# Two attention layers on one core: the first passes' q and k copied straight from the part tile, and TensorE's first scores ahead of the second half's k, v and sums

## The chip, the cores and the metric

The kernel runs on one core of a Trainium2 chip. The metric is the device time of one execution in microseconds. The profile is one execution taken by the hardware profiler; the times named in the text are microseconds from the start of its span.

## The reference, cut to what matters

The input x is (4, 1024, 128) in float32: batch, rows, features. Two attentions with 16 heads of 8 features follow each other, then a choice of 2 of 8 experts.

```python
def _L0_attn_ref(x, Wqkv, bqkv, Wr, br):        # first attention, on _layernorm(x)
    qkv = jnp.einsum('bhce,ef->bhcf', xh, Wqkv) + bqkv
    q, k, v = jnp.split(qkv, 3, axis=-1)
    att = jnp.einsum('bhqe,bhke->bhqk', q, k) / jnp.sqrt(jnp.float32(he))
    mask = jnp.tril(jnp.ones((c, c), dtype=att.dtype), k=-1)
    att = jax.nn.softmax(att * mask, axis=-1)   # masked scores are 0, not -inf
    out = jnp.einsum('bhqk,bhke->bhqe', att, v)
    ...
    return out @ Wr + br
...
    # second attention: rope on q and k inputs, causal softmax, out_proj, layer norm,
    # gates, top 2 of 8 experts, layer norm
x = x + _L0_attn_ref(_layernorm(x, axis=-1), ...)
x = x + _L0_ffn_ref(_layernorm(x, axis=-1), ...)
```

Since the masked scores of the first attention are 0 and not left out, every query also needs the sum of v over all later keys: that is the `suffix` job ("the sums").

## The kernel before, in words

**Slots, stretches, passes, sets, units.** An attention of one batch is a slot; `SLOTS` gives their order, the first attention of batch 0, then of batch 1, then the second attention of batch 0, and so on. A stretch is the stream of scores of one slot. It runs in passes: one half of the queries (512) by four of the 16 heads; the first four passes are those of the first query half. A pass is a row of sets, each set one or two units. A unit is a 128 x 1024 block of scores in a pair of PSUM banks; there are three pairs (`PAIRS`), so unit n uses the banks of unit n - 3. In the first query half a pass has three sets of 2, 2 and 1 units, so set 0 has units 0 and 1, set 1 has 2 and 3, set 2 has 4, set 3 begins pass 1.

**The stream.** For each set TensorE computes scores (line 1309, `heads_scores`), ScalarE takes the exponential of a unit (line 1504), GpSimd masks the blocks on the diagonal (line 1580), and three sets later (`LAG`) TensorE multiplies by v (line 1334, `value_group`). ScalarE copies a pass' result out (line 1429). q and k of a pass lie in `qs` and `ks`, three buffers each (`RING`), signalled by `qs_in`.

**Side work.** Everything else (norms, projections, the second attention's inputs, experts) is cut into turns such as `("p1", 1, "xT", 0)`: work, batch, name, half (p1: the first attention's q, k, v; p2: its output and the second's q, k, v; p3: what follows). A planner, `schedule()`, runs at build time with estimated lengths (`JOB_TIMES`, `TURN_TIMES`) and a clock for each engine, and puts each turn at a point between sets, two points in a set. Every engine carries out its turns in this order, in its own stream, and waits where data isn't there: a turn that waits on TensorE or GpSimd holds up the scores or masks behind it. PSUM results of TensorE jobs are counted by `side_done` and, once read, by `side_free`.

**The front.** What must be ready before the first scores is in a list by hand, `BEFORE_TURNS`, of batch 0: for both row halves j = 0, 1 the statistics (`stats`, `root`), normalised rows (`rows`), transpose (`xT`), `q`, `k`, the stores to DRAM (`parts_out`) and `v`; then the two `suffix` sums; between them `pairs`, `bound` and `roots` of p0, a bound on the scores that ends in a flag, which each engine but GpSimd reads before a stretch. TensorE does all its jobs of the list, then waits for `N_SCORES` reads and for pass 0's data, and begins. Each q and k is split in two float32r parts in the tile `part` (lines 1675 and 1676; for k of this list ScalarE makes the first part, line 1441, and VectorE the second). `parts_out` stores q in four DMAs and k in two; for half 0 the k stores are ScalarE's (line 919). Then SP loads passes 0 and 1 from DRAM (`load(0)`, `load(1)`; it waits until all six stores have landed), where q's parts are each stored twice, and k is read twice, because the scores are products of parts on 64 rows for each head.

**The queues of the front.** SP issues the first rows, `FIRST`, `bv` and `WEIGHTS`, then the turns. ScalarE issues the `NARROW` loads, converts them, then issues `BROADCAST` (eight vectors, then `earlier8` and `bars8`), `cos` and `sin`, and only then carries out its turns, the first of them `roots`.

## Time and profile before

| | |
|---|---|
| median of 3 runs | 789.04 us (788.24 to 795.55) |
| the profiled execution's own time | 789.42 us |
| its span | 787.6 us |
| TensorE matmul, busy | 681.1 us (86%) |
| ScalarE, busy | 648.1 us (82%) |
| VectorE, busy | 395.9 us (50%) |
| GpSimd, busy | 322.9 us (41%) |

The exponentials (128 x 1024, 576 of them, 1124 ns each) are 601.4 us of ScalarE's time; the products with v 322.2 us and the scores 185.1 us of TensorE's. The page also cuts the span into 40 slices of 19.7 us and gives each engine's busy share in tenths:

```profile
PE   4798998988899989989897989989999789999853
PEld 2333333433234333233232333233333233233422
DVE  5355344456445453556244644574345765455573
ACT  1499997999899997999698889998889798888721
POOL 3162235323633434434553245532666314424334
PEclk9589998999999997999898999999999999999976
```

ScalarE (ACT) is busy in one tenth of the first slice, four of the second, and then nine or so until the last slices. PEclk is TensorE's granted clock, in tenths of full speed. A timeline row reads: start, length, engine, line, operation, output and inputs with their shapes, number of merged instructions, and in square brackets the idle time before and what released it.

### The profile page before, as it was taken

The numbers are of one execution on the slowest core, as the hardware profiler recorded it, in microseconds if no ns is written. First come the engines' busy times: TensorE is split into PE (matmuls) and PEld (weight loads), VectorE is DVE, ScalarE is ACT, GpSimd is POOL, SyncE is SP. The second block draws the span as 40 slices with busy tenths as digits, with TensorE's granted clock in tenths as the row PEclk, the third lists the DMA queues.
The fourth block names the chain that finished last, engine by engine and source line by source line (L and its number), as shares of the span: only waits on it lengthen the run. The fifth ranks groups of instructions, "written<-read, shape, count | busy, mean of one in ns | idle before, by whom it ended". The sixth has DMA issues, their size and how long they took to land. (4 is left out here: it accounts for less than half of the span.)

```text
span 787.6 us, 15418 instructions
## 1 busy us (share of the span) xinstructions
PE 681.1 (86%) x5568; PEld 259.9 (33%) x5568; DVE 395.9 (50%) x1062; ACT 648.1 (82%) x721; POOL 322.9 (41%) x635
## 2 busy tenths in 40 slices
PE   4798998988899989989897989989999789999853
PEld 2333333433234333233232333233333233233422
DVE  5355344456445453556244644574345765455573
ACT  1499997999899997999698889998889798888721
POOL 3162235323633434434553245532666314424334
PEclk9589998999999997999898999999999999999976
DMA  6848357535567432424455244423545451230100
GB/s 162 288 136 263 101 202 239 178 127 202 181 213 243 162 110 86 148 83 135 143 163 155 104 141 130 146 83 121 190 151 179 158 162 60 70 96 1 41 13 15
DMA packets 77142, 109.86 MB, mean 139 GB/s; under 512 B 13928, under 2 KB 28400, under 8 KB 77040
## 3 DMA queue, kind: packets, MB, share of 16 engines
q1 hardware_dynamic: 72944, 107.32, 42.8%
q10 hardware_dynamic: 4096, 1.33, 0.8%
q8 instruction: 46, 0.75, 0.4%
q14 instruction: 56, 0.46, 0.2%
HBM read 60.94 MB, written 47.68 MB: 138 GB/s over the span
## 5 line engine op out<-in xcount | busy, mean ns | idle before, releaser
L1504 ACT ACTIVATE probs<-scores,shift 128x1024 f32<-128x1024 f32 x576 | 601.4, 1124 | 80.2 <-PE scores L1309 73.7
L1580 POOL TENSOR_SCALAR_AFFINE_SELECT probs<-probs 128x256 f32<-128x256 f32 (+1 forms) x448 | 197.5, 458 | 379.8 <-ACT probs L1504 379.1
L1334 PE MATMUL acc<-probs,v 128*9 128x512 f32 (+3 forms) x3072 | 322.2, 508 | 10.7 <-ACT num L1429 9.5
L1309 PE MATMUL scores<-qs,ks 32*128 32x512 f32 (+3 forms) x1536 | 185.1, 434 | 41.0 <-ACT probs L1504 37.4
L1309 PEld LDWEIGHTS scores<-qs,ks 32*128 32x128 f32 x1536 | 83.1, 189 | 259.9 <-ACT probs L1504 175.0
L1334 PEld LDWEIGHTS acc<-probs,v 128*9 128x9 f32 x3072 | 59.1, 100 | 132.2 <-issue 72.9
L1627 DVE TENSOR_TENSOR prod<-side,G 128x512 f32<-128x512 f32 x48 | 33.1, 691 | 89.3 <-PE side L1275 79.3
L1275 PE MATMUL side<-we,x1T 128*128 128x512 f32 x100 | 58.6, 669 | 0.8 <-DVE x1T L1916 0.8
L1561 POOL TENSOR_TENSOR moe<-psum 128x256 f32<-128x256 f32 x32 | 24.4, 762 | 51.3 <-DVE x1b L1627 26.6
L1429 ACT ACTIVATE num<-acc 128x512 f32<-128x512 f32 x64 | 38.2, 596 | 5.3 <-PE acc L1334 5.2
L1536 POOL TENSOR_TENSOR rstd<-rstd,expo 128x4 f32<-128x4 f32 x32 | 33.4, 1044 | 2.7
L1660 DVE COPY xT<-side 128x512 f32<-128x512 f32 x22 | 15.2, 691 | 30.2 <-PE side L1148 30.1
L1675 DVE TENSOR_SCALAR part<-side,binqk 128x512 fp32r<-128x512 f32 x16 | 12.0, 751 | 31.4 <-PE side L1154 21.8
L1154 PE MATMUL side<-xT,win 128*128 128x512 f32 x32 | 20.1, 712 | 6.6 <-DVE part L1676 6.6
L1464 ACT ACTIVATE probs<-scores,G 128x128 f32<-128x128 f32 x40 | 11.0, 389 | 15.4 <-PE scores L1275 9.9
L1675 DVE TENSOR_SCALAR part<-side,bqk 128x512 fp32r<-128x512 f32 x12 | 9.0, 751 | 25.0 <-PE side L1154 25.0
L1635 DVE BATCH_NORM_STATS2 stats<-xrow 128x6 f32<-128x128 f32 x72 | 15.6, 279 | 11.8 <-DMA xrow<-in_x 9.5
L1275 PEld LDWEIGHTS side<-we,x1T 128*128 128x128 f32 x100 | 15.5, 195 | 16.1 <-issue 11.4
L1627 DVE TENSOR_TENSOR psum<-prod 128x512 f32<-128x512 f32 x24 | 17.7, 737 | 3.1
L1275 PE MATMUL scores<-we,x1T 128*128 128x512 f32 x28 | 17.4, 767 | 0.0
L1562 POOL TENSOR_TENSOR moe<-moe 128x128 f32<-128x128 f32 x32 | 15.8, 493 | 2.5
L1848 DVE TENSOR_SCALAR sfx<-side,sfx 128x128 f32<-128x128 f32 x28 | 9.8, 351 | 12.6 <-PE side L1235 8.4
(186 smaller groups left out, 602.4 us busy)
## 6 DMA issues: line engine op xcount, KB each, us to landing
ks<-k_dram SPq DMA_DIRECT2D x96, 256.0 KB, 4.1
q_dram<-part SPq DMA_DIRECT2D x64, 256.0 KB, 3.5
qs<-q_dram SPq DMA_DIRECT2D x64, 256.0 KB, 3.2
num_dram<-num SPq DMA_DIRECT2D x60, 256.0 KB, 3.3
k_dram<-part SPq DMA_DIRECT2D x30, 256.0 KB, 4.0
xrow<-in_x SPq DMA_DIRECT2D x16, 256.0 KB, 4.4
nat<-num_dram SPq DMA_DIRECT2D x15, 256.0 KB
rdenb<-rden_dram SPq DMA_DIRECT2D x15, 256.0 KB
```

What stands on the lines that cost most here:

```text
L1154: signal(pe.matmul(out[:, :], w[:, int(name == "k"), :], xT[a][:, a or j, :], start=True, stop=True), last)
L1275: signal(pe.matmul(out[:, :], x1T[i // TH][:, i % TH, :], we[:, first:first + HALF], start=True, stop=True), last)
L1309: ins = pe.matmul(dst, ks[u][r, kt // TH, (kt % TH) * P:(kt % TH + 1) * P], qs[u][r, q0:q0 + w], start=True, stop=not shifted)
L1334: ins = pe.matmul(acc[h * VW:h * VW + VC, q0:q0 + w], v9[V_OF[k]][:, kt, :, HG * hg + h], src, start=(s == 0), stop=last, skip_group_check ...
L1429: act.activation(num[gp % 2][:, :], acc[:, :], ACT.Copy).then_inc(acc_read, 1)
L1504: act.activation(dst, src, ACT.Exp, bias=shift[:, column(st):column(st) + 1], scale=SCALE).then_inc(probs_raw, 1)
L1536: pool.tensor_tensor(r, r, expo[:, 0:1].broadcast_to(list(r.shape)), ALU.pow).then_inc(root_ready[w], 1)
L1561: link(pool.tensor_tensor(moe[:, :, :], psum4[:, i % 2, 0:2, :], psum4[:, i % 2, 2:4, :], ALU.add))
L1562: link(pool.tensor_tensor(moe1[:, :], moe[:, 0, :], moe[:, 1, :], ALU.add))
L1580: ins = pool.affine_select(out=blocks, in_=blocks, compare_op=ALU.is_ge, fill=0.0, base=a - 1, pattern=[[0, blocks.shape[1]], [1, P]], cha ...
L1627: return dve.tensor_tensor(out, in0, in1, op)
L1675: link(dve.tensor_scalar(pt[:, c, 0, :], src, bias[:, c:c + 1], None, ALU.add))
```

## The change

- The list: `rows` of half 0 stands before `pairs`, `q` of half 0 before `roots` (on VectorE).
- `STRAIGHT = 2`: passes 0 and 1 get q and k by DMA from the tile `part` (SBUF) into `qs` and `ks` (SBUF) instead of by way of DRAM. A pass takes four copies of 128 KB: two of q (SP) and two of k (one by SP, one by ScalarE). Pass 0's q copies are issued once `q` is read, the others once `k` is. The stores to DRAM stay, behind the copies; `load(2)` follows them, in place of `load(0)` and `load(1)`.
- `BEHIND`: TensorE's `k` and `v` of half 1 follow set 0's scores, the sums sets 1 and 3. The first part of `k` of half 1 is made by VectorE, not ScalarE. `BEFORE_BANKS` names the banks of the jobs in the list, and `PAIR_FREE` replaces the wait for `N_SCORES` by one for each pair: pair 0 needs `k` of half 0 to be read, pair 2 (set 1) `k` of half 1.
- `earlier8`, `bars8`, `cos` and `sin` leave ScalarE's queue for SP's, behind the second half's `parts_out`, with a semaphore of their own, for which VectorE waits at the first `rope0` and the first `pick0`.
- The planner starts VectorE's and SP's clocks at 5.0, and places no TensorE job before set 4.

```diff
@@ -349,11 +349,16 @@
-BEFORE_TURNS = ([("p1", 0, "stats", 0), ("p1", 0, "root", 0), ("p1", 0, "stats", 1), ("p1", 0, "root", 1), ("p0", 0, "pairs", 0),
-                 ("p1", 0, "rows", 0), ("p1", 0, "xT", 0), ("p0", 0, "bound", 0), ("p1", 0, "rows", 1), ("p0", 0, "roots", 0),
-                 ("p1", 0, "q", 0), ("p1", 0, "k", 0), ("p1", 0, "parts_out", 0), ("p1", 0, "xT", 1), ("p1", 0, "v", 0),
+BEFORE_TURNS = ([("p1", 0, "stats", 0), ("p1", 0, "root", 0), ("p1", 0, "stats", 1), ("p1", 0, "root", 1),
+                 ("p1", 0, "rows", 0), ("p0", 0, "pairs", 0), ("p1", 0, "xT", 0), ("p0", 0, "bound", 0), ("p1", 0, "rows", 1),
+                 ("p1", 0, "q", 0), ("p0", 0, "roots", 0), ("p1", 0, "k", 0), ("p1", 0, "parts_out", 0), ("p1", 0, "xT", 1), ("p1", 0, "v", 0),
                  ("p1", 0, "q", 1), ("p1", 0, "k", 1), ("p1", 0, "parts_out", 1), ("p1", 0, "v", 1), ("p1", 0, "suffix", 1), ("p1", 0, "suffix", 0)])
 PIECES.update(pairs=1, bound=1)
+BEFORE_BANKS = {("p1", 0, "xT", 0): 1, ("p0", 0, "pairs", 0): 0, ("p0", 0, "bound", 0): 2, ("p1", 0, "q", 0): 3, ("p1", 0, "k", 0): 0,
+                ("p1", 0, "xT", 1): 4, ("p1", 0, "q", 1): 5, ("p1", 0, "k", 1): 4}
+BEHIND = {("p1", 0, "k", 1): 0, ("p1", 0, "v", 1): 0, ("p1", 0, "suffix", 1): 1, ("p1", 0, "suffix", 0): 3}
@@ -382,7 +387,7 @@
     pending = sorted(waits, key=late)
-    clock = {"PE": 0.0, "ACT": 0.0, "DVE": 0.0, "POOL": 0.0, "SP": 0.0}
+    clock = {"PE": 0.0, "ACT": 0.0, "DVE": 5.0, "POOL": 0.0, "SP": 5.0}
     banks, jobs, uses = [0.0], [], [x for x in BEFORE_TURNS if x[2] == "q"]
@@ -493,7 +498,7 @@
         others(t, p, False)
-        room = True
+        room = g > max(BEHIND.values())
         if room and open_job is None and banks[-1] <= t and p + 4 < NPOINT:
@@ -575,7 +580,7 @@
 BY_ACT = set(BY_ACT_ORDER)
-K_BY_ACT = [x[:4] for x in BEFORE if x[2] == "k" and x[5]]
+K_BY_ACT = [x[:4] for x in BEFORE if x[2] == "k" and x[5] and x[:4] not in BEHIND]
 TURNS = [x for x in BEFORE + sum(DURING, []) + AFTER if x[5]]
@@ -594,8 +599,7 @@
 N_AFTER = sum(x[2] in PIECES and x[5] for x in AFTER)
-JOB_BANK = [n % (SPARE + 1) if n < N_BEFORE - 2 else SPARE for n in range(N_BEFORE)] + [SPARE] * (len(JOB) - N_BEFORE - N_AFTER)
+JOB_BANK = [BEFORE_BANKS.get(x, SPARE) for x in JOBS[:N_BEFORE]] + [SPARE] * (len(JOB) - N_BEFORE - N_AFTER)
 JOB_BANK += [n % (SPARE + 1) for n in range(N_AFTER)]
@@ -621,6 +625,7 @@
 N_SCORES = max(n for n in range(N_BEFORE) if JOB_BANK[n] < SPARE) + 1
+PAIR_FREE = [max(n for n in range(N_BEFORE) if JOB_BANK[n] // 2 == i) + 1 for i in range(PAIRS)]
 FIRST_FILLS = NVB + 3
@@ -854,10 +860,10 @@
         BROADCAST = [(binv, binv_d), (br, br_d), (bo, bo_d), (bg, bg_d), (l1w, l1w_d), (l1b, l1b_d),
-                     (l2w, l2w_d), (l2b, l2b_d), (earlier8, earlier8_d), (bars8, bars8_d)]
+                     (l2w, l2w_d), (l2b, l2b_d)]
         n_first = len(FIRST)
         n_narrow = len(NARROW)
-        n_weights = len(WEIGHTS) + len(BROADCAST) + 2
+        n_weights = len(WEIGHTS) + len(BROADCAST)
         PARTS_DMAS = 6
@@ -871,9 +877,21 @@
+        STRAIGHT = 2
         def landed(gp):
-            return 16 * sum(pass_dmas(i) for i in range(gp % RING, gp + 1, RING))
+            return 16 * sum(4 if i < STRAIGHT else pass_dmas(i) for i in range(gp % RING, gp + 1, RING))
+        def q_straight(engine, gp, i):
+            src = part[0][32 * gp:32 * gp + 32, 0, i, :].bitcast(F32)
+            engine.dma_start(qs[gp][i::2, :].bitcast(F32), src.unsqueeze(1).broadcast_to([32, 2, HALF])).then_inc(qs_in[gp], 16)
+        def k_straight(engine, gp, i):
+            engine.dma_start(ks[gp][i::2, 0, :].bitcast(F32), part[0][32 * gp:32 * gp + 32, 1, :, :].bitcast(F32)).then_inc(qs_in[gp], 16)
@@ -954,7 +972,7 @@
                 _st, k, qh, hg = PASS_OF[gp]
-                if hg == 0:
+                if hg == 0 or gp == STRAIGHT:
                     wait_stored(k, qh)
@@ -1084,13 +1102,25 @@
             for x in BEFORE:
+                if x[:4] == ("p1", 0, "parts_out", 0):
+                    sp.wait_ge(side_free, done(("p1", 0, "q", 0)))
+                    for i in range(2):
+                        q_straight(sp, 0, i)
+                    sp.wait_ge(side_free, done(("p1", 0, "k", 0)))
+                    k_straight(sp, 0, 0)
+                    for i in range(2):
+                        q_straight(sp, 1, i)
+                    k_straight(sp, 1, 0)
                 if x[5]:
...
                 if x[:4] == ("p1", 0, "parts_out", 0):
-                    load(0)
-                    load(1)
+                    load(2)
+            for t, d in ((earlier8, earlier8_d), (bars8, bars8_d)):
+                sp.dma_start(t[:, :], bc(d)).then_inc(late_weights_in, 16)
+            for t, d in ((cos, cos_d), (sin, sin_d)):
+                sp.dma_start(t[:, :, :], d.rearrange("(t p) f -> p t f", p=P)).then_inc(late_weights_in, 16)
             loads = {}
-            for gp in range(2, NP):
+            for gp in range(3, NP):
                 first = max(PASS_FIRST[gp] - LEAD, PASS_FIRST[gp - RING + 1] if gp >= RING else 0)
@@ -1282,10 +1312,11 @@
                     pe.wait_ge(qs_in[u], landed(gp))
-                if g == 0:
-                    pe.wait_ge(side_free, N_SCORES)
-                elif last >= PAIRS:
+                for unit in UNITS_OF[g]:
+                    if unit < PAIRS:
+                        pe.wait_ge(side_free, PAIR_FREE[unit])
+                if last >= PAIRS:
@@ -1369,8 +1400,14 @@
             for x in BEFORE:
-                turn(*x)
+                if x[:4] not in BEHIND:
+                    turn(*x)
             pe.wait_ge(narrowed, n_narrow)
+            def behind(g):
+                for x in BEFORE:
+                    if BEHIND.get(x[:4]) == g:
+                        turn(*x)
@@ -1378,6 +1415,8 @@
                         scores_set(g, shifted)
+                    if not shifted:
+                        behind(g)
                     for x in DURING[2 * g]:
@@ -1440,6 +1482,9 @@
                 if (work, b, name, i) == ("p1", 0, "parts_out", 0):
+                    act.wait_ge(side_free, done(("p1", 0, "k", 0)))
+                    for gp in range(STRAIGHT):
+                        k_straight(act, gp, 1)
                     k_out(act, 0, b, i)
@@ -1479,8 +1524,6 @@
                 act.dma_start(t[:, :], d.unsqueeze(0).broadcast_to([P, d.shape[0]])).then_inc(weights_in, 16)
-            for t, d in ((cos, cos_d), (sin, sin_d)):
-                act.dma_start(t[:, :, :], d.rearrange("(t p) f -> p t f", p=P)).then_inc(weights_in, 16)
             for x in BEFORE:
@@ -1667,6 +1710,9 @@
                         dve.wait_ge(part_out[use % 2], stored(use - 2))
+                        if use == 2:
+                            for gp in range(STRAIGHT):
+                                dve.wait_ge(qs_in[gp], landed(gp))
                         if a0:
@@ -1870,6 +1916,8 @@
                         n = 2 * b + i
+                        if n == 0:
+                            dve.wait_ge(late_weights_in, 16 * 4)
                         inputs = xn[:, :, :].rearrange("p t (h f two) -> p t h f two", h=H, two=2)
@@ -1972,6 +2020,8 @@
                 if c == 0:
+                    if n == 0:
+                        dve.wait_ge(late_weights_in, 16 * 4)
```

## Rows read from the trace of the kernel before

**Rows 1.** Table of stretches (us; busy us per engine, granted clock, DMA share, GB/s)
```profile
0.00:30.00 30.00, 15.74 (x52) 10.08 (x52) 15.19 (x48) 3.69 (x7) 7.11 (x15) 0.85 0.69 199
30.00:113.00 83.00, 75.54 (x632) 28.02 (x632) 38.26 (x106) 77.70 (x80) 29.89 (x66) 0.91 0.58 183
```

**Rows 2.** Timeline, 8 to 21 us (start, length; q behind an engine: its queue issuing)
```profile
8.85 2.44 ACTq L1481 DMA_DIRECT2D earlier<-in_earlier  x1
...
10.02 3.78 PE L1154 MATMUL scores<-xT,wqkv 128*128 128x512 f32 x4 [0.27 <-DVE xT L1660]
...
13.69 0.60 ACTq L1483 DMA_DIRECT2D sin<-in_sin  x1
...
14.20 1.06 PE L1160 MATMUL side<-wqkv,xT 128*128 128x128 f32 x8
...
14.82 0.17 DVE L1713 TENSOR_SCALAR shift<-ccw 128x4 f32<-128x4 f32 x1 [3.52 <-ACT ccw L1447]
...
15.64 0.73 DVE L1675 TENSOR_SCALAR part<-scores,bqk 128x512 fp32r<-128x512 f32 x1
16.40 1.41 DVE L1676 SCALAR_TENSOR_TENSOR part<-scores,bqk,part 128x512 fp32r<-128x512 f32 x2
...
17.84 2.77 SPq L1004 DMA_DIRECT2D q_dram<-part  x4
```

**Rows 3.** Timeline, 22 to 33 us, the engines
```profile
22.10 1.92 PE L1160 MATMUL scores<-wqkv,xT 128*128 128x128 f32 x8
...
27.89 2.08 PE L1235 MATMUL side<-later,v 128*128 128x128 f32 x8 [1.54 <-DVE sfx L1848]
...
30.15 0.80 PE L1309 MATMUL scores<-qs,ks 32*128 32x512 f32 x4 [0.18 <-issue]
31.06 2.12 ACT L1504 ACTIVATE probs<-scores,shift 128x1024 f32<-128x1024 f32 x2 [8.03 <-PE scores L1309]
```

**Rows 4.** Timeline, 23 to 34 us, SP's queue
```profile
23.92 0.32 SPq L934 DMA_DIRECT2D qs<-q_dram  x1
...
26.13 2.25 SPq L1004 DMA_DIRECT2D q_dram<-part  x4
...
28.43 1.85 SPq L919 DMA_DIRECT2D k_dram<-part  x2
...
32.22 0.33 SPq L934 DMA_DIRECT2D qs<-q_dram  x1
...
33.19 0.59 SPq L1043 DMA_DIRECT2D xrow<-in_x  x1
```

**Rows 5.** Timeline, 37 to 52 us, the stream once it runs
```profile
37.74 0.87 DVE L1635 BATCH_NORM_STATS2 stats<-xrow 128x6 f32<-128x128 f32 x4 [5.89 <-DMA xrow<-in_x]
...
37.99 0.80 PE L1309 MATMUL scores<-qs,ks 32*128 32x384 f32 x8
...
42.07 1.04 POOL L1536 TENSOR_TENSOR rstd<-rstd,expo 128x4 f32<-128x4 f32 x1
...
43.15 1.42 DVE L1642 TENSOR_SCALAR xrow<-xrow,mv,rstd 128x128 f32<-128x128 f32 x4 [1.23 <-POOL rstd L1536]
...
45.45 0.66 PE L1148 MATMUL side<-ident,xrow 128*128 128x128 f32 x4
...
50.83 0.51 PE L1309 MATMUL scores<-qs,ks 32*128 32x384 f32 x8
```

**Rows 6.** View of the DMA issues (count, KB each, median us to landing)
```profile
ks<-k_dram SPq DMA_DIRECT2D x96, 256.0 KB, 4.1
...
xn_dram<-xn SPq DMA_DIRECT2D x8, 256.0 KB, 2.3
```

**Rows 7.** Table of stretches, where v runs fast, and 28 to 44 us
```profile
13.00:15.00 2.00, 2.00 (x13) 1.41 (x11) 0.17 (x1) 0.62 (x3) 0.00 (x0) 1.00 0.78 215
28.00:44.00 16.00, 13.24 (x80) 5.62 (x84) 5.57 (x25) 11.51 (x13) 7.17 (x16) 0.50 0.80 261
```

**Rows 8.** Timeline, ScalarE alone, its longest idle time before 130 us but the first
```profile
124.52 2.12 ACT L1504 ACTIVATE probs<-scores,shift 128x1024 f32<-128x1024 f32 x2 [4.88 <-PE scores L1309]
```

More of the change, by code:

```diff
@@ L785, in build @@
         weights_in = sem("weights_in")
+        late_weights_in = sem("late_weights_in")
         filled = sem("filled")
@@ L1412, in _ @@
                     with pe.If(pe.value_load(flags[0:1, st:st + 1], min_val=0, max_val=1)):
+                        if st == 0:
+                            for g in range(SETS_ALL):
+                                behind(g)
                         exact(st)
```

## The prediction

> **What bounds the kernel now.** I read the page's busy shares first, then the table of stretches, and then the timeline of the first 55 us engine by engine. From 30 to 113 us ScalarE is busy 77.7 of 83 us and TensorE 75.5; before 30 us ScalarE is busy 3.7 of 30 us [rows 1]. ScalarE's exponentials over the scores set the pace from the first scores on, so what counts is when the first exponential starts, and whether the stream behind it then runs dense. It starts at 31.06, behind the first scores at 30.15 [rows 3].
>
> The front chain has two parts. First, VectorE is idle for 3.52 us before 14.82: it waits for two small ScalarE operations which stand behind DMA issues in ScalarE's queue. Those issues run back to back from the `earlier` one at 8.85 (2.44 us) to `sin`, which ends at 14.29 [rows 2]. So the first half's q, finished on TensorE at 11.9 (two of the four matmuls that begin at 10.02, 3.78 us together), is read only from 15.64, and k's second part ends at 16.40 + 1.41 = 17.81 [rows 2]. Second, from 17.84 four q stores (2.77 us) are issued, the loads wait until they have landed (23.92) [rows 2, 4], and TensorE meanwhile does the second half's q and k, v and the two sums over v; the last ends at 27.89 + 2.08 = 29.97 [rows 3]. Copies landing early would buy nothing alone: loads issued at 23.92 to 24.9 with 4.1 us to landing [rows 4, 6] are there by 29.0, so TensorE's own order is what ends last, by 1 us. The change attacks both.
>
> **ScalarE's queue, and the first k.** Removed from that queue: `earlier`, `bars`, `cos`, `sin`, 5.4 us of issue (8.85 to 14.29). ScalarE then does the two small operations as soon as the bound is there, near 10. VectorE's new order puts the first half's q ahead of `roots`. I go on from the old times (pulling `rows` ahead of `pairs` may give 0.2 us more; I leave it out). q is on TensorE until 11.9; VectorE's two operations (0.73, and half of 1.41) give 13.4; the `roots` group (14.82 to about 15.7) lasts 0.9, to 14.3. k's matmuls end at 13.8, ScalarE's half of k takes about as long as one of VectorE's operations, to 14.5, and VectorE's residual of about 0.75 ends at 15.3 [rows 2]. k is free at 15.3 instead of 17.8.
>
> **The straight copies.** Pass 0 needs two q copies (issued from 13.4) and two k copies, one from each queue, at 15.3. Before does not show a copy from SBUF to SBUF. Bounds from the nearest rows: 2.3 us to landing for xn's store and 4.1 for a k load, both 256 KB against 128 KB here [rows 6]. I take 2.3, since half the bytes go and no pass load competes. That gives 17.6; with 4.1 it gives 19.4. The Trainium skill (DMA: Bandwidth & Descriptors, Anatomy of one DMA) gives some 2.0 us fixed plus bytes over 436 GB/s, so an estimated 2.3 us, most of it the receipt of the last write and heaviest for HBM; by that the copies would also be in at 17.6.
>
> TensorE must first do xT 1 and v 0 (the latter ends 14.20 + 1.06 = 15.3), and q 1, which waits for VectorE's copy of xT 1 until 16.0. Its two matmuls take 1.9 us (half of 3.78), or an estimated 1.1 at the pace told below [rows 2]. It ends at 17.1 to 17.9. With a little for the branch, the first scores stand at 18.1 instead of 30.15: **12.0 us earlier**. The other bound of the copy makes it 10.8.
>
> **What now stands behind the first scores.** k 1 and v 1 go after set 0, the sums after sets 1 and 3. Set 1 uses the pair of banks that k 1 was in, so it waits for TensorE's k and VectorE's two reads of it (ScalarE no longer helps). In the trace TensorE shows two paces: v takes 1.06 us with the clock granted at 1.00 (2.4 GHz), and 1.92 later, the pace of 0.50 (1.2 GHz); before, TensorE paused behind v 0 until the second half's q; now that pause is at most 1.3 us, so I lean to the fast pace [rows 2, 3, 7].
> At the fast pace: set 0 0.5, k 1.1, reads 1.5, so set 1 at 21.3; v read by 22.3; sum 1 to 23.4, read by VectorE to 24.9; set 3 meanwhile; sum 0 to 26.0; values of set 0 1.1; set 4 at 27.1. That is 9.0 us from set 0 to set 4 against 30.15 to 37.99, 7.8 us, before [rows 3, 5]: a loss of 1.2. At the slow pace (0.8, 1.9, then v 1.9, sums of 2.1, values 1.9) set 4 comes at 31.8, a loss of 5.9.
>
> **SP's queue, what is late next.** SP now issues, in order: six straight copies (two of them by 14.4, four from 15.3, some 0.5 each, to 17.2), four q stores to 20.0, pass 2's load when these have landed (3.3 us after the last issue, as 20.61 to 23.92), so 23.3 to 24.2, the second half's six stores (4.1 us, 26.13 to 30.28 before) to 28.4, then the four moved loads. Their price is 0.5 each where the queue is free (`sin` 0.60) and up to 2.44 where it backs up: 2.0 us in all, or up to 5.4 [rows 2, 4]. I take 2.0: 30.4. Between the last store's issue (30.28) and the next issue (32.22) SP takes 1.9 us for its branch: 32.3. Then pass 3's load (1.0) and, since the planner's SP clock starts at 5 and so puts them at set 3, the next batch's rows at 33.3, where they stood at 33.19 [rows 4]. **ScalarE is 12 us earlier, the next batch's rows are not.** They are read 4.55 us after issue (33.19, 37.74), so at 37.9; statistics an estimated 1.3 (0.87 and the aggregates), GpSimd's root 1.3 (1.04 and one small operation), VectorE's rows 1.4: 42.0, where they ended at 44.57 before [rows 4, 5]. Behind the waiting root stand GpSimd's masks, and behind the waiting transpose (45.45) TensorE's whole stream.
>
> The offset of 5 us moves the transpose from set 7 to about set 9 or 10. Unhindered, set 10 (50.83 before [rows 5]) would stand at 50.83 - 12.0 + 1.2 = 40.0. With the transpose just behind set 9: 42.0 + 0.7 + 0.8 for values = 43.5; one set later: about 42.5. I take 43.0, which is **7.8 us** earlier than before. At the slow pace 44.7 would be reached without waiting, 6.1 us. The wait so caps the gain and makes the clock count for little. Pass 3's load, landed at 37.4, is needed for set 9 near 37: hidden within the same wait. Moving `cos`, `sin` and the two tables costs their users nothing: by the code's order the first use (`rope0`) comes four passes and the round trip of their sums later.
>
> That such a ring backs up shows in the 2.44 us that `earlier` took to issue, against 0.60 for `sin` [rows 2]. The Trainium skill (DMA: Bandwidth & Descriptors, Queues, rings and completion order) says that on each engine the descriptors of one queue are consumed in ring order; `cos` and `sin`, of many small runs, now stand in SP's ring ahead of pass 3 and the rows. By that the sum would lose what they still occupy when the rows are issued, an estimated 0.8 us, to 7.0. No run here shows yet what they occupy.
>
> **The sum.** 12.0 - 1.2 - 3.0 (wait for the rows) = 7.8 us off the profiled execution, whose device time was 789.42 (span 787.6): 781.6. The runs' median is 0.38 lower, so 781.2.
>
> **Rivals.**
> *A, the rows are no hindrance* (transpose placed at set 11 or later, or rows read sooner): the gain is 10.8, 778.2. For it: transposes have slack by the offset. Against: SP's count above.
> *B, slow clock and slow copies*: 10.8 - 5.9 = 4.9, 784.1. For it: granted 0.50 from 28 to 44 us [rows 7].
> *C, SP backs up*: the moved loads at 5.4 instead of 2.0 make the rows 3.4 us later, so a gain of 4.4, 784.6. For it: `earlier` with 2.44. Against: the weights then all competed.
> *D, slower*: side work is placed anew over the whole kernel, and TensorE, in order, waits for one late operand. Such a wait costs 4.88 us where it happened (ScalarE without scores until 124.52 [rows 8]). One new one leaves 2.9 us (786.1); from the second on the gain is gone (2 x 4.88 = 9.8, 2.0 us slower, 791.0). To be slower by over 1%, four are needed. Equally, such waits may vanish (down to 776).
> *E, the change does not do what it says* (the first scores held by something unseen, gain under 2 us): 788.
>
> **Chances.** Forecast (6 to 9 us gained) 0.46; A 0.17; B and C together 0.22; D 0.11; E 0.04. The range 776.0 to 787.0 takes in one lost or one won wait and leaves out about 0.15. About 1%, 7.9 us, is what a measurement of this kernel can tell from no change. The forecast lies just at that line: half of its chance, A, and the happy side of D's reshuffle give faster 0.47; B, C, E, and the other half give within 1% 0.49; several new waits give slower 0.04.
>
> **What would show it.** Right: ScalarE's idle before its first exponential ends near 19; k's part is free near 15.3; the copies land 2 to 3 us after issue; a gap of ScalarE between the first two and the next exponentials of about 0.5 to 2 us; SP issues the next batch's rows at 32 to 34, and TensorE's first transpose in the stream is preceded by an idle time, released through VectorE's rows. Wrong: first scores later than 20; set 4 past 30; no wait at that transpose; idle times of over 3 us of ScalarE past 60 us that before does not have.

## The result

The change makes the kernel a little slower. Over 20 runs of each the ratio of the changed kernel to the kernel before is 1.0084 (95% interval 1.0055 to 1.0113), against the forecast 781.2 us, 1.0% faster. The medians of all runs are 799.96 and 789.15 us; the first holds some disturbed runs, which the ratio leaves out. The profiled execution took 793.76 us, with a span of 791.9 instead of 787.6. The page's first and second part after:

```profile
span 791.9 us, 15419 instructions
...
PE   4789988987888998998997989989988799899954
...
ACT  1869989998769987999899979998889788888621
...
PEclk9969999999979998999999989999999899999976
```

ScalarE's second slice is fuller, 8 instead of 4: the front did move. TensorE's stays at 7. The weak slices now are the third (6) and the eleventh and twelfth (7, 6).

**The front**, timeline after (start, length, engine, what; in brackets the idle time before and its releaser). The rows answer to [rows 2, 3, 5]:

```profile
14.43 0.75 DVE L1722 SCALAR_TENSOR_TENSOR part<-scores,bqk,part 128x512 fp32r<-128x512 f32 x1 [0.17 <-ACT part L1483]
...
15.21 1.46 ACTq L894 DMA_DIRECT2D ks<-part  x2
...
20.01 0.50 PE L1340 MATMUL scores<-qs,ks 32*128 32x512 f32 x4 [3.05 <-DMA ks<-part]
...
20.64 2.12 ACT L1547 ACTIVATE probs<-scores,shift 128x1024 f32<-128x1024 f32 x2 [6.32 <-PE scores L1340]
...
28.97 0.51 PE L1340 MATMUL scores<-qs,ks 32*128 32x384 f32 x8
```

k is read at 15.18, as worked out (15.3). The k copies are issued at 15.21, and TensorE, which waits for nothing else, stands idle for 3.05 us until they have landed: scores at 20.01, the first exponential at 20.64 instead of 31.06, 10.4 us earlier. Set 4 is at 28.97.

**Then the rows of the next batch**, which answer to [rows 4, 5]:

```profile
35.85 0.59 SPq L1061 DMA_DIRECT2D xrow<-in_x  x1
...
40.11 0.87 DVE L1678 BATCH_NORM_STATS2 stats<-xrow 128x6 f32<-128x128 f32 x4 [10.18 <-DMA xrow<-in_x]
...
43.22 1.52 DVE L1685 TENSOR_SCALAR xrow<-xrow,mv,rstd 128x128 f32<-128x128 f32 x4
...
44.88 1.09 PE L1178 MATMUL side<-ident,xrow 128*128 128x128 f32 x4 [3.25 <-DVE xrow L1685]
...
48.99 1.11 ACT L1547 ACTIVATE probs<-scores,shift 128x1024 f32<-128x1024 f32 x1 [5.19 <-PE scores L1340]
```

They are issued at 35.85 (33.19 before), read at 40.11, and TensorE stands idle for 3.25 us before their transposes; ScalarE gets nothing for 5.19 us.

**Where the gain goes** is best seen unit by unit. From ScalarE's rows of the timeline I took the start of each of the 576 exponentials (a row that merges n of them split evenly) and subtracted the same unit's start in the kernel before; microseconds, minus is earlier. The columns other than the first are runs told below.

```
unit  after  plan_alone  front_old_plan  before_clocks_2_5
   0  -10.4        -1.5           -10.8               -0.4
   9  -10.3        -1.8            -6.6               -0.4
  18   -9.7        -2.4            +3.2               -0.1
  24   -3.0        -1.3            +3.2               +0.0
  60   -2.2        -0.6            +3.2               +1.1
  96   -4.7        -1.0            +2.5               -3.0
 132   -2.4        +0.8            +2.2               +0.0
 156   +0.5        +6.9            +2.5               +6.7
 168   +6.6       +11.0            +2.1               +9.2
 276   +8.6       +13.8            +2.0              +11.0
 300   +3.8        +9.0            -1.6               +6.5
 336   +0.8        +6.0            -1.7               +3.5
 420   +2.6       +10.1            -1.5               +3.4
 575   +2.6       +14.6            -1.9               +3.4
```

Three parts: 10 us earlier up to unit 18; 7 us of it lost by unit 24, the wait for the rows; and between units 96 and 276 another 13.3 lost, in small steps and one large one, of which 7.8 come back by unit 336. The stream ends 2.6 us later than before, and the tail behind it takes 1.7 longer. The later steps are not where the change is. But the planner's new start (clocks at 5, no TensorE job before set 4) places 230 of 582 turns elsewhere, in all of the first four stretches up to unit 288, and none behind. That is where the curve moves.

One column is to be read with care: `plan_alone`'s profile is the slowest of its six executions (803.8 us, where their median is 797.66). Its second rise, from 6.0 at unit 336 to 14.6 at the end, lies where no turn was moved and stands in no other column, so I don't put it down to the arrangement.

### The profile page after: what moved, and what is told of

It reads as the page before. It is cut to its first block and busy times, and to the rows that moved or that the text cites. A ratio compares the mean times of both kernels' runs of the same rounds, so it can differ in the third digit from the quotient of the medians.

```text
span 791.9 us, 15419 instructions
## 1 busy us (share of the span) xinstructions
PE 675.3 (85%) x5568; PEld 258.5 (33%) x5568; DVE 398.6 (50%) x1063; ACT 648.3 (82%) x720; POOL 322.8 (41%) x635
## 3 DMA queue, kind: packets, MB, share of 16 engines
q10 hardware_dynamic: 1888, 1.52, 0.8%
## 5 line engine op out<-in xcount | busy, mean ns | idle before, releaser
L1623 POOL TENSOR_SCALAR_AFFINE_SELECT probs<-probs 128x256 f32<-128x256 f32 (+1 forms) x448 | 199.7, 464 | 389.4 <-ACT probs L1547 389.0
L1340 PE MATMUL scores<-qs,ks 32*128 32x512 f32 (+3 forms) x1536 | 182.2, 427 | 46.3 <-ACT probs L1547 37.6
L1340 PEld LDWEIGHTS scores<-qs,ks 32*128 32x128 f32 x1536 | 81.5, 185 | 257.5 <-ACT probs L1547 172.0
L1678 DVE BATCH_NORM_STATS2 stats<-xrow 128x6 f32<-128x128 f32 x72 | 15.6, 279 | 14.8 <-DMA xrow<-in_x 12.6
L1184 PE MATMUL side<-xT,win 128*128 128x512 f32 x32 | 17.9, 643 | 4.7 <-DVE xT L1703 4.0
L1305 PEld LDWEIGHTS side<-we,x1T 128*128 128x128 f32 x100 | 15.3, 193 | 17.6 <-issue 12.6
L1685 DVE TENSOR_SCALAR xrow<-xrow,mv,rstd 128x128 f32<-128x128 f32 x32 | 12.7, 458 | 5.5 <-POOL rstd L1579 5.4
```

The source lines that it names most:

```text
L1184: signal(pe.matmul(out[:, :], w[:, int(name == "k"), :], xT[a][:, a or j, :], start=True, stop=True), last)
L1305: signal(pe.matmul(out[:, :], x1T[i // TH][:, i % TH, :], we[:, first:first + HALF], start=True, stop=True), last)
L1340: ins = pe.matmul(dst, ks[u][r, kt // TH, (kt % TH) * P:(kt % TH + 1) * P], qs[u][r, q0:q0 + w], start=True, stop=not shifted)
L1623: ins = pool.affine_select(out=blocks, in_=blocks, compare_op=ALU.is_ge, fill=0.0, base=a - 1, pattern=[[0, blocks.shape[1]], [1, P]], cha ...
L1678: ins = dve.bn_stats(stats[w][:, TH * j + t, :], src[:, t, :])
```

## The experiments

**The arrangement or the front: each alone.** `front_old_plan` is the changed kernel with

```diff
-    clock = {"PE": 0.0, "ACT": 0.0, "DVE": 5.0, "POOL": 0.0, "SP": 5.0}
+    clock = {"PE": 0.0, "ACT": 0.0, "DVE": 0.0, "POOL": 0.0, "SP": 0.0}
...
-        room = g > max(BEHIND.values())
+        room = True
```

> The changed kernel with the planner's start put back (all clocks 0, TensorE jobs allowed from the start): all side work of the stream stands where it stood in the kernel before; list, copies, queues and the jobs behind the first scores are the changed kernel's. Theory P (the rearranged side work of the first four stretches costs some 10 us): the first exponential again near 20.6, the transpose waits for the rows until about 45, where it stood before, so 0 to 3 us are left of the front's gain at unit 60, and the end keeps them: 786 to 789, ratio 0.996 to 1.000. Theory F (the front itself, by its other phase against the transfers, costs it later): 792 to 797, as the changed kernel.

`plan_alone` is the kernel before with the planner's two lines changed instead.

> The kernel before with only the planner's start changed (VectorE's and SP's clocks at 5.0, no TensorE job before set 4), so that all side work stands as in the changed kernel. Theory P: the stream loses 8 to 11 us between units 96 and 276 against the kernel before and gives about 5 back: 793 to 800, ratio 1.005 to 1.014. Theory F: 788 to 790, no difference.

Measured: `front_old_plan` 787.68 us, ratio 0.996 (0.9922 to 0.9997); `plan_alone` 797.66 us, ratio 1.0112 (1.006 to 1.0164). The two curves in the table run in parallel from unit 96 to 276: the changed kernel rises by 13.3 there, `plan_alone` by 14.8, `front_old_plan` falls by 0.5. With the front alone the kernel is a shade faster; the arrangement alone makes it slower by as much as the whole change (1.0112 against 1.0084, the intervals overlap). Theory P holds, theory F falls.

**Is it this arrangement, or any?** `before_clocks_2_5` is the kernel before with both clocks at 2.5: 218 turns elsewhere, the first transpose where it was.

> The kernel before, where the planner starts VectorE's and SP's clocks at 2.5 instead of 0: 218 of 582 turns of the stream stand elsewhere, the first transpose does not. Theory P1 (any rearrangement of this kind has a price of its own, by which late operands TensorE then meets): a difference of several us of either sign, with steps at single units. Theory P2 (only the changed kernel's late transposes cost): within 0.3% of before, 788 to 791, as the first transposes stand where they stood.

Measured: 792.45 us, ratio 1.003 (0.9995 to 1.0066). The table's last column: 3 us ahead at unit 96, level at 132, 9.2 behind at 168 and 11.0 at 276, in steps at single units, as theory P1 has it. So a nudge of the planner moves places in the middle of the kernel by some 10 us, most of which is made up again later, and the late first transposes are not what costs. By the ratio the sum of it is not told from nothing.

**One meeting taken out.** The largest step after is at units 156 to 168, +6.1 us. The timeline after at that place:

```profile
216.66 4.11 DVE L1685 TENSOR_SCALAR xrow<-xrow,mv,rstd 128x128 f32<-128x128 f32 x4 [2.02 <-POOL rstd L1579]
...
217.22 1.26 POOL L1586 TENSOR_TENSOR sq<-part 128x512 bf16<-128x512 f32 x1
...
218.44 1.89 POOL L1587 TENSOR_TENSOR sq<-part 128x1024 bf16<-128x1024 f32 x1
...
220.92 1.09 PE L1178 MATMUL side<-ident,xrow 128*128 128x128 f32 x4 [3.39 <-DVE xrow L1685]
...
225.03 1.11 ACT L1547 ACTIVATE probs<-scores,shift 128x1024 f32<-128x1024 f32 x1 [5.04 <-PE scores L1340]
```

Four operations of VectorE that took 1.42 us in [rows 5] take 4.11 while GpSimd makes the squares `sq`; TensorE waits 3.39 us for them, ScalarE 5.04. In the kernel before, the squares stand three sets before these rows; of the five profiles that I searched (before, after, and the three runs above) only the changed kernel and `plan_alone` have such a row over 2 us. So do the three runs below that keep the new arrangement and leave the squares where they are (4.11, 4.11 and 4.10 us). The view of the tile `xrow` from 216 to 222 us (duration in ns: shortest, median, longest) shows the four apart:

```profile
L1685 DVE TENSOR_SCALAR xrow<-xrow,mv,rstd x4: 436/989/1929, 216.7 to 220.3; 128x128 f32<-128x128 f32 x4
```

The longest, 1929 ns, begins at 218.48 beside GpSimd's 1.89 us operation at 218.44; the one before it, 1.32 us from 217.24, lies beside GpSimd's 1.26 us at 217.22. `after_sq_later` moves that one turn by a set:

```diff
+_sq = next(x for x in DURING[171] if x[:4] == ("p2", 1, "sq", 0))
+DURING[171].remove(_sq)
+DURING[173].append(_sq)
```

> The changed kernel with one GpSimd turn moved by one set: the squares of the second work's batch 1, half 0, stand after set 86 instead of set 85, where VectorE normalises the first attention's last batch. Theory Q (the 6 us lost between units 156 and 168 come from this meeting: VectorE's four operations took 4.11 us beside GpSimd's squares and TensorE waited 3.39 us for them): the four operations take 1.1 to 1.7 us, the wait is under 1 us, the loss there 0 to 2 us instead of 6; the end 786 to 792, ratio 0.996 to 1.004. Rival (the wait has another cause, or is made up by the next late operand): loss there 4 us or more.

```profile
217.06 1.53 DVE L1688 TENSOR_SCALAR xrow<-xrow,mv,rstd 128x128 f32<-128x128 f32 x4 [2.03 <-POOL rstd L1582]
...
218.74 0.63 PE L1181 MATMUL side<-ident,xrow 128*128 128x128 f32 x4 [0.81 <-DVE xrow L1688]
...
222.71 0.47 PE L1202 MATMUL side<-headsum,sq 128*128 128x16 bf16 x12 [1.59 <-POOL sq L1590]
```

The four operations take 1.53, the wait is 0.81; but TensorE now waits 1.59 for the squares in `norm`. The step from unit 156 to 168 is 3.2 instead of 6.1. Time: 795.64 us, ratio 1.009 (1.0052 to 1.0128), no better. At unit 276 it is 3.7 us ahead of the changed kernel, at unit 575 only 0.4. So taking the meeting out gives back 2.9 us at its place, and nothing at the end: later waits take it back. The time I expected was wrong.

**What holds the stream at set 7.** My step said: the rows' load, behind SP's work. `front_old_plan_rows_early` and `after_rows_early` load these rows right behind the straight copies,

```diff
                     k_straight(sp, 1, 0)
+                    for i in range(2):
+                        turn("p1", 1, "load", i)
```

> As the first, and SP loads the second batch's rows (1.2 us of issue) right behind the straight copies instead of inside the stream. Theory P with the wait for the rows as the second loss: rows ready near 30, the transpose at set 7 waits for nothing, the difference to before at unit 60 is -8 to -10, and stays: 779 to 782, ratio 0.988 to 0.992. If the wait at the transpose was not the rows' load: no better than the first. Theory F: above 787.

> The changed kernel with the second batch's rows loaded right behind the straight copies. At unit 60 the difference to before should be -9 to -10 instead of -2.9. Theory P: the stretches after it still lose some 10 us, and the end is 785 to 790. Theory F says the same of the end; this run tells only whether the 7 us lost by unit 24 come back when the rows are early.

Under the old plan the wait is longer: in the table `front_old_plan` is 10.8 us ahead at unit 0 and 3.2 behind at unit 18, since the transposes stand at set 7 there. Measured: 785.23 us, ratio 0.9941 (0.9908 to 0.9974), and 797.5, ratio 1.0116 (1.0052 to 1.0179). Both expectations were missed: at unit 60 the first run stands at +1.8 us (expected -8 to -10), the second at -3.8 (expected -9 to -10). With the old arrangement a little is won, but the wait stayed: ScalarE is still idle for 8.78 us before 47.58. With the rows in place by then, the next thing in VectorE's queue, the x rows of the second work, was late; and pass 3's load in the other run. So I put all of SP's front in the order of need (`sp_reordered_old_plan`: rows, x rows, pass 3, then the second half's stores, the late weights behind set 12).

> The changed kernel with the side work of the kernel before, and SP's order changed by what the rows-early trace shows: SP issues the second batch's rows and the first x rows of the second work behind pass 2's load, then pass 3's load, and only then the second half's stores; the four late weights go behind set 12. Theory S (SP's backlog, each transfer in its turn, is what takes the front's gain; not one load alone): rows ready by 36, wait at the transpose under 3 us, difference to before at unit 24 is -5 to -9, kept to the end: 780 to 785, ratio 0.988 to 0.994. Theory R (something else holds the stream to the old time, near 45 to 50 us): unit 24 within 2 us of before, 787 to 790.

Measured: 788.1 us, ratio 0.9966 (0.9931 to 1.0002). Theory R: unit 24 at +0.5 us. The timeline of that run:

```profile
26.73 1.14 SPq L1061 DMA_DIRECT2D xrow<-in_x  x2
...
30.09 0.23 DVE L2128 COPY later_count<-count 128x128 f32<-128x128 f32 x1
...
36.31 0.87 DVE L1687 BATCH_NORM_STATS2 stats<-xrow 128x6 f32<-128x128 f32 x4 [6.00 <-issue]
...
42.65 1.09 PE L1187 MATMUL side<-ident,xrow 128*128 128x128 f32 x4 [7.56 <-DVE xrow L1694]
```

The rows are issued at 26.73 and, at the 4 us or so of such loads, there by 31; VectorE's last work is over at 30.3; yet it starts on them at 36.31, after 6.00 us of idle time that the view gives to issue. In the kernel before an idle time of about that length, 5.89 us, stood there, put down to the load [rows 5]. What VectorE does in between is to read the flag and jump over the exact path's code. The same gap is already in the second of the two runs above, where these rows were loaded early:

```profile
28.86 0.23 DVE L2121 COPY later_count<-count 128x128 f32<-128x128 f32 x1
...
34.31 0.87 DVE L1680 BATCH_NORM_STATS2 stats<-xrow 128x6 f32<-128x128 f32 x4 [5.22 <-issue]
```

It stands at the start of the other stretches too: in the kernel before, nine idle times of 2.76 to 5.14 us put down to issue. Its second stretch:

```profile
113.70 0.22 DVE L2069 COPY later_count<-count 128x128 f32<-128x128 f32 x1
118.53 0.69 DVE L1627 TENSOR_TENSOR xrow<-xrow,br 128x512 f32<-128x512 f32 x1 [4.62 <-issue]
```

and TensorE's wait that follows is ScalarE's 4.88 us before 124.52 [rows 8], the very row from which I had priced a late operand.

**VectorE's branch left out.** In these three runs VectorE has neither flag reads nor the exact path (that part of the computation, for large scores, is left out on VectorE):

```diff
...
-                    with dve.If(dve.value_load(flags[0:1, st:st + 1], min_val=0, max_val=1)):
-                        exact(st)
...
```

> The kernel before, but VectorE doesn't read the flag at the ten stretch starts and has no code for the exact path (so the path for large scores is left out on VectorE; the other engines keep theirs). Theory V (VectorE is held 3 to 6 us at each stretch start by the read of the flag and the jump over the exact path's code, idle that the view puts down to issue; TensorE then waits for VectorE's side work): the statistics of the second batch start when its rows land, near 37.5 in this kernel still; the idle times of VectorE after 113, 203, 287, 377 and 471 us vanish, and with them ScalarE's of 4 to 5 us near 124 and 386: 10 to 20 us faster, ratio 0.975 to 0.988. Rival (those idle times are waits for data that the view does not name): they stay, ratio 0.997 to 1.003.

> The changed kernel without VectorE's flag reads and exact path. Theory V with P (the rearranged side work costs because other jobs meet the held VectorE at the stretch starts): statistics of the second batch still wait for their rows until about 40, but the loss between units 132 and 168 is gone: difference to the one above -2 to +2 us at the end, ratio to the kernel before 0.975 to 0.99. P alone (the arrangement costs by other waits): it stays 6 to 10 us above the run above.

> The run with SP's order changed and the side work of before, now without VectorE's flag reads and exact path. Theory V: VectorE starts the second batch's statistics as soon as its last sum is read, near 31 instead of 36.31; the transpose at set 7 waits 0 to 3 us instead of 7.56; difference to the kernel before at unit 24 is -6 to -9, and at the end it is 5 to 9 us below the first run of this call: ratio to the kernel before 0.965 to 0.98. Rival: statistics again near 36.

| run | median us | ratio to before | interval |
|---|---|---|---|
| before_no_dve_branch | 770.03 | 0.9782 | 0.9733 to 0.983 |
| after_no_dve_branch | 778.57 | 0.9875 | 0.984 to 0.991 |
| reordered_no_dve_branch | 762.41 | 0.9707 | 0.9658 to 0.9755 |

The last one's timeline, where VectorE now goes on at once:

```profile
30.30 0.23 DVE L2128 COPY later_count<-count 128x128 f32<-128x128 f32 x1
30.60 1.12 DVE L1687 BATCH_NORM_STATS2 stats<-xrow 128x6 f32<-128x128 f32 x4
...
36.69 1.09 PE L1187 MATMUL side<-ident,xrow 128*128 128x128 f32 x4 [1.40 <-DVE xrow L1694]
```

Statistics at 30.60 instead of 36.31, transposes at 36.69 instead of 42.65. The differences to the kernel before, in us:

```
unit  after  front_old_plan  sp_reordered_old_plan  reordered_no_dve_branch  before_no_dve_branch
   0  -10.4           -10.8                  -11.0                    -10.8                  -4.3
   9  -10.3            -6.6                   -9.9                     -9.7                  -5.0
  18   -9.7            +3.2                   +0.5                     -7.3                  +1.7
  24   -3.0            +3.2                   +0.5                     -7.3                  +1.7
  60   -2.2            +3.2                   +0.4                     -7.3                  +1.7
 168   +6.6            +2.1                   +2.2                    -12.9                  -0.1
 300   +3.8            -1.6                   -1.4                    -23.2                 -10.3
 575   +2.6            -1.9                   +0.2                    -30.5                 -18.4
```

Without the branch the reordered front is 7.3 us ahead at unit 24 and keeps it; with the branch it was not ahead at all. And the changed kernel is slower than the kernel before, branch or none: 778.57 against 770.03. The hope that the branch explains that price falls.

Two rows of these runs bear on what held VectorE at the front. The first is from `after_no_dve_branch`, the second from `before_no_dve_branch`:

```profile
39.37 1.12 DVE L1678 BATCH_NORM_STATS2 stats<-xrow 128x6 f32<-128x128 f32 x4 [10.97 <-DMA xrow<-in_x]
```

```profile
37.60 1.12 DVE L1635 BATCH_NORM_STATS2 stats<-xrow 128x6 f32<-128x128 f32 x4 [9.97 <-DMA xrow<-in_x]
```

With no branch there, both still wait for the load. In the changed kernel the load was the holder, as forecast: VectorE's gap began at 29.93 and, at the 5.2 to 6.5 us measured at this place in the runs with early rows, would have ended by 36.5, while the rows were read at 40.11, and at 39.37 without the branch; and `after_no_dve_branch` stands at -2.7 us at unit 24, where the changed kernel stands at -3.0. In the kernel before the two run side by side: the gap, from 31.85, would end at 37.1 to 38.4, and the rows are read at 37.74, so which ended last no run tells. The jump is what holds the stream once the rows are early.

**The jump or the read.** `before_fall_through`, `reordered_fall_through` and `after_fall_through` leave nothing out. VectorE's normal path is laid out as TensorE's was: nested blocks that are fallen through, the exact path behind them with a second copy of the stream.

```diff
...
+            with ExitStack() as good_stretches:
+                for st in range(last):
+                    begin(st)
...
+                    dve.reg_mov(flagged, dve.value_load(flags[0:1, st:st + 1], min_val=0, max_val=1))
+                    good_stretches.enter_context(dve.If_eq(flagged, 0))
+                    rest(st)
+                tail()
...
+            with dve.If_ne(flagged, 0):
...
```

> The kernel before with the same flag reads on VectorE, but the normal path laid out without a jump (as TensorE's is: the whole stream stands in nested blocks that are fallen through, and the exact path with a second copy of the stream stands behind it). Theory J (the jump over the exact path's code costs, the read little): nearly all of the gain of leaving the branch out stays: ratio 0.977 to 0.984. Theory L (the read of the flag costs): 0.99 to 1.0, VectorE's idle times after 113 and 287 us stay at 3 us or more.

> The changed front with the side work of before, SP's order changed, and VectorE's normal path without a jump; nothing is left out. Theory J: as without the branch, 0.970 to 0.977 of before, some 760 to 770 us; the transpose at set 7 waits 1 to 3 us, the difference to before at unit 24 is -6 or more. Theory L: 0.985 to 0.995.

> The changed kernel, its side work untouched, with VectorE's normal path without a jump. Against the kernel before with the same layout (0.9712) the change should still be worth nothing or less if the rearranged side work is its price: ratio to before 0.975 to 0.988; the meeting at unit 156 to 168 still costs some 5 to 6 us. If the jump was what made the change a loss: 0.960 to 0.970.

| run | median us | ratio to before | interval |
|---|---|---|---|
| before_fall_through | 766.47 | 0.9712 | 0.967 to 0.9754 |
| reordered_fall_through | 762.92 | 0.9664 | 0.9606 to 0.9723 |
| after_fall_through | 780.2 | 0.989 | 0.9844 to 0.9936 |

Theory J: the whole gain stays, and the first two runs came out below the ratios that I gave them, the third just above. `before_fall_through` at the place shown above:

```profile
111.92 0.22 DVE L2068 COPY later_count<-count 128x128 f32<-128x128 f32 x1
113.36 0.69 DVE L1627 TENSOR_TENSOR xrow<-xrow,br 128x512 f32<-128x512 f32 x1 [1.23 <-issue]
```

1.23 us instead of 4.62: with the read kept and the block fallen through some 1.2 us stay, and 3.4 go with the jump. What in the jump takes the time no run here shows. `reordered_fall_through` is the fastest complete kernel of this study, 3.4% under the kernel before. How much of that its front adds is less sure than the jump's part: the intervals of the first two overlap. `after_fall_through` is slower than the kernel before with the same layout (0.989 against 0.9712, intervals apart). So the jump did not make the change a loss; without it the change still costs 1.8%. Its step from unit 156 to 168 is again 5.5 us, within the 5 to 6 expected.

**The copies without the new order.** `no_behind` is `front_old_plan` with `BEHIND = {}`: all of TensorE's jobs ahead of the first scores again.

> The changed kernel with the side work of the kernel before and TensorE's jobs all ahead of the first scores again (only the freed queues, the list's order and the straight copies stay). My step 'the copies alone buy nothing, TensorE's order ends last by 1 us': first exponential at about 27 (before's 31.06 less 2.5 for k and 1 for TensorE at its faster pace), the difference at unit 24 is then 0 to -3 us and the end 786 to 790. If the copies gated the front instead: first exponential near 20.6 as in the changed kernel.

Measured: 789.81 us, ratio 0.9994 (0.9959 to 1.0029).

```profile
25.35 0.32 SPq L952 DMA_DIRECT2D qs<-q_dram  x1
...
25.66 2.07 PE L1265 MATMUL side<-later,v 128*128 128x128 f32 x8 [1.54 <-DVE sfx L1894]
...
27.67 0.80 PE L1340 MATMUL scores<-qs,ks 32*128 32x512 f32 x4
...
28.59 2.12 ACT L1547 ACTIVATE probs<-scores,shift 128x1024 f32<-128x1024 f32 x2 [8.43 <-PE scores L1340]
```

TensorE goes from the last sum, which ends at 27.73, to the first scores without idle time: it didn't wait for passes 0 and 1, and its own order ends last, as the prediction said. The first exponential is 2.5 us earlier, not 10.4. The time is within the range that I gave; unit 24 is not: 2.5 us later than in the kernel before, where I expected 0 to 3 us earlier.

## Why the prediction was wrong, by its own steps

- **ScalarE's queue, k free at 15.3**: right, 15.18.
- **The straight copies**: a mis-sized term. I took 2.3 us, from xn's store; the view of the DMA issues after (count, KB, median us to landing):

```profile
qs<-part SPq DMA_DIRECT2D x4, 128.0 KB, 3.6
ks<-part SPq DMA_DIRECT2D x2, 128.0 KB, 4.1
ks<-part ACTq DMA_DIRECT2D x2, 128.0 KB, 4.6
```

  3.6 us for q and 4.1 to 4.6 for k, against an upper bound of 4.1, though only half the bytes; TensorE begins 4.8 us after the k copies' issue at 15.21. The reason 'half the bytes' was worth nothing, and 'no pass load competes' was little help: from 13 to 20 us the DMA engines are busy for 0.93 of the time, and all that is issued in that stretch are these copies and the stores behind them. The first scores came 10.1 us earlier (20.01 instead of 30.15), not 12.0; the other bound (10.8) was the nearer one.
- **What stands behind the first scores**: right. Set 0 to set 4 takes 20.01 to 28.97, 9.0 us, as summed at the fast pace.
- **SP's queue**: near. The four moved loads took 2.4 us (30.74 to 33.11), where 2.0 was taken; but the stores behind the copies took longer (3.81 for four), and the next rows were issued at 35.85, not 33.3. What `cos` and `sin` occupy in SP's ring no run tells apart.
- **The wait for the rows**: place and kind right, size wrong. Up to set 10 the stream kept its lead: that set's scores stand at 40.83, as the 'unhindered' 40.0 had it, 10.0 us earlier than before. The transposes stand behind set 10, and the wait fell on set 11, whose exponential is at 48.99 instead of 53.49: 4.5 us earlier, and 3.0 at unit 24, where 7.8 was forecast. Two terms were too small. The rows' normalising ended at 44.74, not 42.0, which is SP's lateness (35.85 instead of 33.3) handed on. And the transposes and values behind it took 2.85 us (44.88 to 47.73), not 1.5, at the slow pace. The table of stretches after shows TensorE's clock granted at 0.50 (1.2 GHz) in 40 to 50 us:

```profile
30.00:40.00 10.00, 7.45 (x84) 2.47 (x76) 0.00 (x0) 9.53 (x11) 3.00 (x7) 0.94 0.80 220
40.00:50.00 10.00, 6.69 (x52) 2.52 (x44) 7.36 (x27) 4.37 (x5) 7.55 (x15) 0.50 0.55 185
```

  In finer stretches it is 1.00 up to 38.5 us and 0.50 from 39.0 to 52.0: it fell right behind the 1.52 us in which TensorE stood idle before 38.53, and the wait for the rows came on top.
- **"The wait so caps the gain and makes the clock count for little"**: half right. The cap held; but what stands behind the wait ran at the slow pace, 1.4 us at set 11.
- **"7.8 us off the profiled execution"**: the step that failed. The sum carried the difference at set 10 to the end unchanged, as if the stream behind were the same. It was not: the planner's clocks are in the diff, and 230 turns moved. By the two profiles the forecast missed by 12.1 us (7.8 earlier forecast, 4.3 later measured): 4.8 of it were gone by unit 24, 5.6 went in the stream behind, 1.7 in the tail. Rival D had the mechanism and the sign, with a chance of 0.11, and I had said that waits as often vanish; the arrangement alone is 1.1% slower (1.0112, 1.006 to 1.0164). The range ended at 787.0 because it took in one such wait and no more. Even with the old arrangement the sum would have missed: `front_old_plan` is at 787.68, since its transposes stand at set 7 and the wait before them took what was left of the front's 10.8 us.
- **Pass 3's load hidden in the same wait**: not quite. It came first, with 1.52 us of TensorE's idle before 38.53, though ScalarE, which had scores in hand, stood idle for only 0.47 us behind it.

What stays open: which meetings make up the arrangement's 10 us. One was shown (3 us at its place, taken back by later waits). Also the first exponential of kernels with the very same front varies from profile to profile: 31.06 in the kernel before, 29.59 in `plan_alone`, 30.69 in `before_clocks_2_5`, 26.77 without the branch; so a few of the front's 10.4 us may be that of one execution. In the ten profiles with the new front and the jobs behind the first scores it lies between 19.62 and 20.64.

## What to carry to other kernels

Where a planner places work at build time, a change of its start is a change of the whole kernel: price it by its own run, with the rest left as it was, before a front's gain is carried to the end. Put the front's steps and the arrangement in separate changes; here the first was worth 0.4% (ratio 0.996) and the second cost 1.1%. And an engine whose idle time is put down to 'issue' may be held by its own instruction stream, behind a wait that hides it: take the wait away and the gap appears. Lay the normal path out so that it is fallen through.

## What the runs showed of the hardware

- VectorE stood idle for 2.8 to 6.0 us where it reads a flag and jumps over a long block (nine places of the kernel before, among them 4.62 us before 118.53; 6.00 before 36.31 in `sp_reordered_old_plan`), and for 1.2 to 1.5 where the same read is followed by code that is fallen through (1.23 before 113.36 in `before_fall_through`, 1.53 before 32.89 in `reordered_fall_through`). Laying the ten places out so was worth 2.9% of the kernel (0.9712).
- Beside GpSimd's squares (1.26 and 1.89 us) VectorE's four 128x128 operations took 4.11 us in all, one set away from them 1.53. Two of the four took 1.32 and 1.93 us. The Trainium skill (SBUF — State Buffer, Who interferes with whom) says that a VectorE instruction in a two-port mode, which `tensor_scalar` can enter, and one of GpSimd shut each other out of a shared pair of SBUF ports for the whole instruction; the trace agrees in kind, as these two lasted about as long as GpSimd's 1.26 and 1.89 us. Which mode they ran in no run here shows.
- A copy of 128 KB from SBUF to SBUF took 3.6 to 4.6 us to land here (medians), no less than the loads of 256 KB from DRAM in the same execution (3.5 for q, 4.3 for k). The Trainium skill (DMA: Bandwidth & Descriptors, Anatomy of one DMA) fits its 2.0 us plus bytes over 436 GB/s to DMAs that GpSimd issues. For these copies, issued by SP and ScalarE, the estimate of 2.3 us worked out from it was too low.
